# Load order, barrier and the preparation step at the start of a four-layer kernel

## The reference, cut to what matters

```python
    x = L0_attn_x
    xn = _layernorm(x, axis=-1)
    x = x + _L0_attn_ref(xn, ...) + _L0_ffn_ref(xn, ...)
...
        def _mqa(x, wqkv, bqkv, w_attn_out, b_attn_out):
            qkv = x @ wqkv + bqkv
...
        def _mamba(x, w_in, conv_w, conv_b, w_xproj, w_dt, b_dt, A_log, Dp, w_out):
            xr = x @ w_in
...
            delta = jax.nn.softplus(x_dbl[..., :DT_RANK] @ w_dt + b_dt)
            A = -jnp.exp(A_log)
...
    def _L0_ffn_ref(x, gate_w, gate_b, w1, w2):
        logits = jnp.einsum('bsd,ed->bse', x, gate_w) + gate_b
        probs = jax.nn.softmax(logits, axis=-2)
        vals_t, idx_t = jax.lax.top_k(probs.transpose(0, 2, 1), K)
```

## Time and profile before

| | |
|---|---|
| median of 3 runs | 2742.13 us (2737.71 to 2745.82) |
| the profiled execution | 2738.4 us |
| its span, first to last instruction | 2737.1 us |
| busy: PE, DVE, ACT, POOL | 81%, 73%, 51%, 30% of the span |
| mean granted TensorE clock | 0.926 of full speed |
| first instruction that needs loaded data | 17.55 us after the span's start |
| first instruction of layer 0 (L1028) | 22.33 us |
| first scores (L679) | 38.95 us |

### The profile page before, as it was taken

How to read it: one execution, slowest core, us unless ns; L and a number is a source line. 1 busy time by engine, 2 the same in 40 slices (tenths; PEclk the granted TensorE clock), 3 DMA queues, 4 the chain that set the end, 5 groups by cost and what they waited for, 6 DMA issues and landing times.

```text
span 2737.1 us, 46943 instructions
## 1 busy us (share of the span) xinstructions
PE 2218.0 (81%) x17922; PEld 1564.0 (57%) x18077; DVE 1987.8 (73%) x4099; ACT 1401.9 (51%) x3576; POOL 819.3 (30%) x460
## 2 busy tenths in 40 slices
PE   4777887777774779999999999778898876888886
PEld 2445554555442646666666666546565555666665
DVE  3389899989888527777777777656666625888887
ACT  1355555555554127777776767424343333545453
POOL 0034334343345102323332323200000002555553
PEclk9899999998987869999999999989999997989988
DMA  2077787777789920000000000000100003445553
GB/s 79 18 183 190 174 197 176 182 183 181 178 196 227 291 86 1 1 1 1 1 1 2 1 1 1 22 13 23 31 21 8 6 26 124 143 169 164 172 175 115
DMA packets 108863, 257.78 MB, mean 94 GB/s; under 512 B 11744, under 2 KB 49888, under 8 KB 108128
## 3 DMA queue, kind: packets, MB, share of 16 engines
q1 hardware_dynamic: 106592, 250.58, 33.8%
q0 software_dynamic: 2048, 4.20, 0.5%
HBM read 236.40 MB, written 17.81 MB: 93 GB/s over the span
## 4 chain that ended last, share of the span: by engine, by line
PE 49%; DVE 22%; ACT 12%; issue 8%; DMA 7%; SPq 1%; POOL 0%; another core or an unknown queue 0%; POOLq 0%; DVEq 0%; ACTq 0%
DMA h<-dtu_rows 6%; PE psum L324 3%; PE psum L683 3%; DVE h L1487 3%; PE psum L679 3%; PE psum L490 3%; ACT pr L1831 3%; PE psum L731 3%; PE psum L570 3%; ACT dA L1783 2%; PE psum L615 2%; PE psum L401 2%; PE psum L690 2%; PE psum L428 2%; ACT pt L1875 2%
## 5 line engine op out<-in xcount | busy, mean ns | idle before, releaser
L2074 POOL TENSOR_TENSOR h<-h,Crep 128x1024 f32<-128x1024 f32 x128 | 322.4, 2520 | 566.7 <-DVE h L1487 566.7
L2058 POOL TENSOR_TENSOR pr<-pr,rsum 128x512 f32<-128x512 f32 x192 | 236.0, 1236 | 547.0 <-DVE rsum L1368 547.0
L1487 DVE TENSOR_TENSOR_SCAN h<-dA,h 128x1024 f32<-128x1024 f32 x128 | 305.0, 2385 | 16.8 <-ACT dA L1971 16.7
L1402 DVE TENSOR_REDUCE mx<-psum 128x4 f32<-128x1024 f32 (+1 forms) x192 | 230.2, 1216 | 106.5 <-PE psum L688 106.5
L1875 ACT ACTIVATE pt<-psum 128x1024 f32<-128x1024 f32 x192 | 189.0, 1020 | 143.8 <-PE psum L690 143.7
L1971 ACT ACTIVATE dA<-dA,A 128x255 f32<-128x255 f32 x512 | 215.7, 499 | 74.9 <-DMA dA<-delta_rows 74.5
L2108 POOL TENSOR_TENSOR h<-h,Crep 128x1024 f32<-128x1024 f32 x64 | 179.7, 2809 | 220.0 <-DVE h L1293 219.7
L1831 ACT ACTIVATE pr<-psum,nb 128x256 f32<-128x256 f32 (+1 forms) x512 | 210.5, 429 | 15.5 <-DVE nb L1360 14.5
L1841 ACT ACTIVATE prT<-psum 128x512 f32<-128x512 f32 x192 | 116.1, 604 | 148.7 <-PE psum L584 146.7
L1480 DVE TENSOR_TENSOR h<-h,psum 128x1024 f32<-128x1024 f32 x128 | 153.1, 1208 | 43.0 <-DMA h<-dtu_rows 42.8
L490 PE MATMUL psum<-h,pack_wf 128*128 128x256 f32 x512 | 162.8, 474 | 15.9 <-POOL h L2108 15.9
(11 more groups left out here) (331 smaller groups left out, 5028.5 us busy)
## 6 DMA issues: line engine op xcount, KB each, us to landing
dA<-delta_rows SPq DMA_DIRECT2D x128, 512.0 KB, 8.1
h<-dtu_rows SPq DMA_DIRECT2D x128, 512.0 KB, 8.7
Brep<-bc_rows SPq DMA_DIRECT2D x64, 512.0 KB, 4.1
Crep<-bc_rows SPq DMA_DIRECT2D x64, 512.0 KB, 5.5
w1r<-m_w SPq DMA_DIRECT2D x32, 256.0 KB, 6.4
w2r<-m_w SPq DMA_DIRECT2D x32, 256.0 KB
dtu_rows<-dtu SPq DMA_DIRECT2D x64, 64.0 KB, 1.7
delta_rows<-delta SPq DMA_DIRECT2D x64, 63.8 KB, 2.0
```

What stands on the lines that cost most here:

```text
L1402: ve.e.tensor_reduce(mx[:, qb, 2 * h:2 * h + 2, groups[0]:groups[-1] + 1], k.psum[:, base:base + 2, :].rearrange("p i (n x) -> p i n x", n ...
L1487: ve.e.tensor_tensor_scan(flat(h), flat(k.dA[n % NDA]), flat(h), 0.0, ALU.mult, ALU.add).then_inc(*k.set("scanned", 0, n))
L2058: po.e.tensor_tensor(p3, p3, bcast(k.rsum[n][:, 0:len(heads[r])], P * (q + 1), 2), ALU.mult).then_inc(*k.set("normed", 1, b, p, r))
L2074: po.e.tensor_tensor(h[:, :, :], h[:, :, :], bcast(k.Crep[b % 2][:, :], 4, 1), ALU.mult).then_inc(*k.set("hC", 0, n))
```

## The change

- `load` issues the DMAs in another order: x of batches 0 and 1 alone (`x0`, 256 KB), `wf`, `wf0`, `wb`, `wfc`, and then the other 1792 KB of x. Each has a semaphore of its own.
- PE, DVE and ACT wait for `x0`, `wf` and `wf0` alone; POOL waits for none. The memsets and ACT's table load stand ahead of these waits. The barrier behind `load` is gone.
- The preparation is split into `prepare_pe`, `prepare_ve` and `prepare_ac`, which stand behind batch 0's first steps on each engine. PE and ACT then wait for `prepared`, which the last `w_tap` on DVE raises. DVE waits for `wb`, `wfc` and the rest of x there.
- Batch 0 has no fill matmuls any more; `identb` and `mask` are not there yet at that place.
- The program of DVE is built ahead of that of PE, because the casts name the tiles that PE reads; this moves nothing.

```diff
--- before.py
+++ after.py
@@ -170,7 +170,7 @@
         return t
 
 
-LAYER_END = ("load", "layer0", "experts0", "layer1", "layer2")
+LAYER_END = ("layer0", "experts0", "layer1", "layer2")
 ENGINES = ("pe", "ve", "ac", "po", "sp")
 
 
@@ -307,7 +307,7 @@
         "ve_first": (0, 4, 5, 16, 17, 21, 22)},
 }
 
-LOADS = {"x": 0, "wf": 1, "wb": 2, "wf0": 3, "wfc": 0, "wf0e": 0, "wf1": 1, "wf2": 2, "wf3": 3}
+LOADS = {"x0": 0, "wf": 1, "wb": 2, "wf0": 3, "wfc": 4, "x": 5, "wf0e": 0, "wf1": 1, "wf2": 2, "wf3": 3}
 
 
 
@@ -352,7 +352,8 @@
     k.pre_read = ("qk_ve", 0, b, 1)
     yield
     bk = pe_take(k, 0)
-    pe_idle(k, bk, 2)
+    if b:
+        pe_idle(k, bk, 2)
     pe.wait_ge(*k.at("gv", b))
     for q in range(QT):
         i = pe.e.transpose(bk[:, q * E0:(q + 1) * E0], k.PT[:, b, q * P:(q + 1) * P], w["ident"][0:E0, 0:E0])
@@ -2341,40 +2342,57 @@
 
 
 def load(k, packs):
-    w, ve, sp, ac = k.w, k.ve, k.sp, k.ac
-    sp.e.dma_start(k.X[:, :, :], k.ins["x"].rearrange("(t p) d -> p t d", p=P)).then_inc(*k.set(*landed("x"), by=16))
-    for pname, t in packs:
-        sp_load(k, pname, t)
-    for pname, t in packs:
-        for q in (k.pe, ve, ac, k.po):
-            q.wait_ge(*k.at(*landed(pname)))
-    ve.wait_ge(*k.at(*landed("x")))
-    for n, t in k.small:
-        ve.e.tensor_copy(t[:, :], w[n])
-        w[n] = t[:, :]
-    pe, bk = k.pe, k.bank[0]
-    for m in range(CI):
-        i = pe.e.matmul(bk[:, m * DI:(m + 1) * DI], w["w_dtin"][:, m * P:(m + 1) * P], w["w_dt"], start=True, stop=True)
-    i.then_inc(*k.set("dt", "weights"))
-    ve.wait_ge(*k.at("dt", "weights"))
-    ve.e.tensor_copy(flat(k.w_step), bk[:, :])
-    ac.e.preload_act_table_set("natural_log_exp_and_others")
-    ac.e.activation(k.A[:, :, :], w["A_log0"], ACT.Exp).then_inc(*k.set("A_exp", 0))
-    ve.wait_ge(*k.at("A_exp", 0))
-    ve.e.tensor_scalar(k.A[:, :, :], k.A[:, :, :], -1.0, None, ALU.mult)
-    for x in k.x1T:
-        ve.e.memset(x[:, 0:CONV - 1], 0.0)
-    for j in range(CONV):
-        ve.e.tensor_tensor(k.w_tap[:, j, :, :], w["w_in"][:, 0:CI, :], w["conv_rows"][:, j, :, :], ALU.mult)
-    for v in k.v:
-        ve.e.memset(v[:, :, :, 9:], 0.0)
-        k.ve.e.memset(v[:, :, :, 8:9], 1.0)
+    w, ve, sp, ac, pe = k.w, k.ve, k.sp, k.ac, k.pe
+    packs = dict(packs)
+    x = k.ins["x"].rearrange("(t p) d -> p t d", p=P)
+    sp.e.dma_start(k.X[:, 0:2 * QT, :], x[:, 0:2 * QT, :]).then_inc(*k.set(*landed("x0"), by=16))
+    for pname in ("wf", "wf0", "wb", "wfc"):
+        sp_load(k, pname, packs[pname])
+    sp.e.dma_start(k.X[:, 2 * QT:, :], x[:, 2 * QT:, :]).then_inc(*k.set(*landed("x"), by=16))
     k.po.e.memset(k.h[0][:, :, :], 0.0).then_inc(*k.set("rows_zero"))
     sp.wait_ge(*k.at("rows_zero"))
     sp.e.dma_start(k.delta_rows.rearrange("i c (m r) s t -> (i c m) (r s t)", r=1), flat(k.h[0])).then_inc(*k.set("delta_stored0", "zero", by=16))
     sp.wait_ge(*k.at("delta_stored0", "zero"))
-    for q in (k.pe, ve, ac, k.po, sp):
-        phase_end(k, q, "load")
+    ac.e.preload_act_table_set("natural_log_exp_and_others")
+    for x in k.x1T:
+        ve.e.memset(x[:, 0:CONV - 1], 0.0)
+    for v in k.v:
+        ve.e.memset(v[:, :, :, 9:], 0.0)
+        ve.e.memset(v[:, :, :, 8:9], 1.0)
+    for q in (pe, ve, ac):
+        for pname in ("x0", "wf", "wf0"):
+            q.wait_ge(*k.at(*landed(pname)))
+
+
+def prepare_ac(k):
+    ac = k.ac
+    ac.e.activation(k.A[:, :, :], k.w["A_log0"], ACT.Exp).then_inc(*k.set("A_exp", 0))
+    ac.wait_ge(*k.at("prepared"))
+
+
+def prepare_pe(k):
+    pe, w = k.pe, k.w
+    for m in range(CI):
+        i = pe.e.matmul(k.bank[0][:, m * DI:(m + 1) * DI], w["w_dtin"][:, m * P:(m + 1) * P], w["w_dt"], start=True, stop=True)
+    i.then_inc(*k.set("dt", "weights"))
+    pe.wait_ge(*k.at("prepared"))
+
+
+def prepare_ve(k):
+    ve, w = k.ve, k.w
+    ve.wait_ge(*k.at(*landed("wb")))
+    for n, t in k.small:
+        ve.e.tensor_copy(t[:, :], w[n])
+        w[n] = t[:, :]
+    ve.wait_ge(*k.at("dt", "weights"))
+    ve.e.tensor_copy(flat(k.w_step), k.bank[0][:, :])
+    ve.wait_ge(*k.at("A_exp", 0))
+    ve.e.tensor_scalar(k.A[:, :, :], k.A[:, :, :], -1.0, None, ALU.mult)
+    ve.wait_ge(*k.at(*landed("wfc")))
+    for j in range(CONV):
+        i = ve.e.tensor_tensor(k.w_tap[:, j, :, :], w["w_in"][:, 0:CI, :], w["conv_rows"][:, j, :, :], ALU.mult)
+    i.then_inc(*k.set("prepared"))
+    ve.wait_ge(*k.at(*landed("x")))
 
 
 def turn0(k, t, e, pre, out, wide, inner, states, results, summing=None):
@@ -2391,10 +2409,12 @@
 
 def layer0(k, t0e):
     k.slot_read, k.pre_read = [None] * 4, None
-    for e, pre, first in (("pe", pe_pre0, pe_first_max), ("ve", ve_pre0, ve_first_max)):
+    for e, pre, first, prepare in (("ve", ve_pre0, ve_first_max, prepare_ve), ("pe", pe_pre0, pe_first_max, prepare_pe)):
         run(pre(k, 0))
+        prepare(k)
         merge(FIRST[0], (first(k, 0), e + "_first"), (pre(k, 1), e + "_pre0"))
     run(ac_pre0(k, 0))
+    prepare_ac(k)
     run(ac_pre0(k, 1))
     ac_max_taken(k, 0, 0)
     sp_negmax(k, 0, 0)
```

## The result

The changed kernel took 2729.0 us (median of 8 runs, 2725.62 to 2734.15), the kernel before 2738.49 beside it (8 runs, 2735.84 to 2745.82). The ratio is 0.9962, with a 95% interval of 0.995 to 0.9975: 10.4 us less, and the interval reaches from 6.8 to 13.7 us. The forecast was 2730.7 us and 11.4 us less. All ratios in this document leave out one slow run, prep_front's of 7503.29 us at a granted clock of 0.405.

A forecast was written before the change was run, and what follows sets the result against it. The prediction took the slack-free chain at the kernel's head as what the change can move: -14.05 (loads) - 0.96 (fill) + 3.63 (preparation) = -11.4 us, from 2742.1 to 2730.7 us; range 2723 to 2739.

The forecast's parts named there:

- What bounds the kernel: Start of the kernel: a line of dependent work without slack; starting batch 0's norm earlier moves all that follows.
- When the data are there: Loads for batch 0: landed at 8.15, so its norm starts at 8.3 in place of 22.33, -14.05 us.
- The skill's price for the same loads: First loads: 2.0 us fixed plus bytes at 436 GB/s, landing at 6.9; the prediction kept the trace rows instead.
- SP held at its second issue: Rival, SP's first issues: the 5.46 us hold stays, norm at 13.4, gain only 6.2 us, 2735.9 us; chance 10%.
- Landings not separated: Rival, first loads: DMA engines share all queued transfers, `wf0` lands at 17.5, gain 2.0 us, 2740.1 us; chance 4%.
- The fill: Batch 0's steps: without the two fill matmuls the turn of the gate's values starts earlier, -0.96 us.
- The preparation: Ahead of batch 0's first scores: weight matmuls, casts, `w_step` and taps now stand on the path, +3.63 us.
- POOL's memset: DVE's casts: the first took 1.04 us beside this memset; away from it 0.21, casts 1.45 us instead of 1.9.
- The clock: PE up to batch 0's maxima: matmuls may change clock level, plus or minus 2 us, taken as zero.
- gives back part: Rival, PE's long layers: a mean clock of 0.9238 costs 3.2 us, result within 0.3%; chance 11%.
- the other clock rival: Long layers: a mean clock of 0.913 or less costs 19.6 us, ending slower at 2750.4 or more; chance 3%.
- The number: Whole kernel: -11.4 us from the median 2742.1, forecast 2730.7 us, 0.42% less.

The follow-up runs named there:

- prep_front: Changed kernel with the preparation ahead of batch 0's steps again, its wait for the rest of x moved behind them; ratio to the kernel before 0.9971.
- wf_second: Changed kernel issuing x0, `wf0`, `wf` in that order; no run time given, batch 0's norm starts at 7.9 to 8.1 us.
- x_first: Changed kernel with all of x issued ahead of the packs again, in two DMAs; ratio to the kernel before 0.9981.
- hold_all: Changed kernel with SP waiting for `wf0` to land before issuing `wb`, `wfc` and the rest of x; no run time given, norm at 9.58 us.
- no_fill: Kernel before with batch 0's fill matmuls removed; no run time given, norm to first scores 15.64 us (16.62 before).
- fold: Changed kernel with the preparation folded into batch 0's idle time; ratio to the kernel before 0.9951.
- x0_last: Changed kernel issuing `wf`, `wf0`, x0 in that order; no run time given, batch 0's norm starts at 7.9 to 8.1 us.
- wf0_first: Changed kernel issuing `wf0`, x0, `wf`; single run 2713.5 us; the same kernel timed again (suffix _timed) took 2725.8 us, ratio to the kernel before 0.9949.
- hold_x: Changed kernel with only the rest of x and the zeros waiting for `wf0` to land; no run time given, `wf0` not landing earlier.

## Why the prediction was right, point by point

- *What bounds the kernel.* That the head has no slack and all that follows moves with it was right, and is the part that the table shows, within its intervals.
- *When the data are there.* This term was mis-sized: -14.05 forecast, -12.56 measured. The step that failed is the rate after x0: I used 423 GB/s for `wf` and `wf0` from 3.6 on, and in the changed order the engines move 200 to 308 from 3 to 6. I had tested the model on the order of before, where `wf` has x ahead of it, but not `wf0` behind two short transfers. A second error hides part of the first: I had 86 KB moved by 3.0, as before, but the changed kernel moved 20 KB from 1 to 2 and then this:

```profile
2.00:3.00 1.00, 0.00 (x0) 0.00 (x0) 0.00 (x0) 0.02 (x1) 0.00 (x0) 1.00 0.98 298
```

  With 318 KB by 3.0 my own rate and tails give a norm at 7.5; so the start was 0.76 us better than forecast, and the rate after it cost 2.25 us. The forecast 8.3 fits the three other orders (7.85 to 8.21 measured), but there too it fits partly by luck: wf_second moves 350 GB/s from 2 to 3 and then 332 to 393, not 86 and then 423.
- *The skill's price for the same loads.* The estimate by the Trainium skill, page "DMA: Bandwidth & Descriptors", section "Anatomy of one DMA", was a landing at 6.9 us; the measured 9.64, and 7.7 to 8.1 in the other orders, lie above it. The forecast of 8.15 from the rows came nearer. But the 2.85 us that I set against the page's 2.0 was no reading of a row: its first part, 1.9 us, came from spreading the 86 KB back at 283 GB/s. The first bytes of x move between 2.4 and 2.6, some 1.7 us after its issue, and those of x0 between 1.8 and 1.9, 1.1 us after 0.74.
- *SP held at its second issue.* The rival was wrong, and for the reason given: `wf` and `wf0` took 0.96 us with 512 runs ahead, 5.78 in x_first with x's list ahead, and the store of zeros 10.84 behind it in the changed kernel. The length of the list alone does not set the time, as the last section says.
- *Landings not separated.* Wrong: x0 landed at 3.3, `wf` at 4.95, `wf0` at 9.64, `wb` at 11.35. hold_all shows that what is queued behind does not delay `wf0`.
- *The fill.* -0.96 forecast, -0.97 in the changed kernel and in no_fill.
- *The preparation.* +3.63 forecast, 3.60 - 0.06 = +3.54 measured, and fold takes 3.6 back. In detail PE and DVE did not arrive together: the casts took 1.16 us (25.28 to 26.44), less than the 1.45 that I had summed, since neighbours overlap, and DVE waited 0.36 for PE. PE's 2.07 us set the term, which is why the sum held.
- *POOL's memset.* The cast of `identb` took 0.22 us in its new place; beside the memset it had taken 1.04. No run moves the memset alone, so the cause is argued. It agrees with the Trainium skill, page "SBUF — State Buffer", section "SBUF: two separate sides", by which some DVE operations and GpSimd lock each other out of one shared pair of ports for a whole instruction.
- *The clock.* I took zero, plus or minus 2 us. In the changed kernel the first group of q of batch 1 took 2.07 us where before it took 1.13, so it runs at 1.2 GHz there. The level is read from the length: the column of the granted clock says 1.00 in both kernels at these groups and also at those of 2.08 us in batch 0, and the same length stands beside 0.50 at 47 to 49. From the first scores to the maxima turned it is 25.12 us (24.65 before); over the thirteen profiles of this study, with the same matmuls there, it runs from 23.1 (no_fill) to 26.0 (fold, x0_last). That is the plus or minus, and it has no sign of its own. The mean clock of the 8 runs of the changed kernel was 0.920 to 0.927. Their mean, 0.9235, lies at the 0.9238 that I had named for the rival "gives back part", and yet the gain stayed above 8.2 us: the kernel before has the same mean clock, 0.9234 to 0.9235 in each of the three groups of its runs beside the experiments (9, 17 and 21 runs). The 0.926 of its profiled execution, from which the rival's price was worked out, was above its own average. A mean of 0.913 was never seen, so the other clock rival did not come true either. That the start differs between executions agrees with the rule of the Trainium skill, page "TensorE: Matmul & The Clock Gate", section "What's actually happening"; of the 27 us that its 1% would leave open, these 3 us, over twelve different kernels, are what was seen. The one kernel that was profiled twice (wf0_first and wf0_first_timed) took 25.08 and 25.63 us.
- *The number.* -12.56 - 0.97 + 3.54 = -9.99 at the first scores, and -9.5 (medians) to -10.4 (ratio) at the end. The forecast time, 2730.7, is 1.7 us above the measured one. The kernel before has a median 3.6 us lower over 8 runs than over the first 3, and the gain is 1.9 us smaller by medians; the two errors partly cancel, so that the forecast time came within 1.7 us is in part luck. The profiled executions (2738.4 and 2725.6) differ by 12.8, which is no better than any two single times are.

## What to carry to other kernels

Where a kernel starts with one line of dependent work, price the line to its first long stretch from the trace; here six kernels carried that shift to the end one to one, as far as intervals of 3.4 to 5.2 us to each side can tell. Issue first what the first steps need. If several such transfers are needed, profile more than one order of them: here the order with both short-run transfers ahead of the largest one was 1.4 us or more behind the three others. Keep a transfer with thousands of short runs behind all issues that someone waits for. Work that must be done once belongs in the idle time of the first steps rather than ahead of or behind them: the trace of before shows that time already.

## What the runs showed of the hardware that I had not expected

- With both transfers of short runs (x0 in 512-byte runs, `wf` in 1188-byte rows) ahead of the 1326.5 KB of `wf0`, the three were there 1.4 us or more later than in any of the other three orders (9.58 to 10.84 against 7.85 to 8.21). The first packets of `wf0` took about 1.55 us each there and 0.51 in wf_second (estimates from the queue's rows). The cause is open, and so is a difference between chips.
- A DMA with thousands of short runs holds its issuing engine at the next issues: 5.46 us behind x's 4096 runs, 10.84 us for the one behind its 3584 runs and `wb` and `wfc`. In hold_x, where 0.7 of the 1.2 MB of `wb` and `wfc` have moved before x's rest is issued at 9.98, the same zeros behind the same 3584 runs are held for 4.83 us only. In all thirteen profiles the held issue ends 3.3 to 3.8 us before the long transfer lands (7.18 and 10.9 before, 15.11 and 18.67 in the changed kernel): the hold ends at about the same distance from the landing, whatever stands ahead of the list, and so it grows with all that is queued ahead. It is the issuer's time only, which matters if the next issue is needed.
